# A four-layer graph network kernel: neighbour rows added in PSUM by VectorE, relation one-hots on ScalarE, two node tiles moved from the dense to the gathered side

## The reference

```
# layer 1, twice; nbrs holds the 32 neighbours of every node
h = crelu(h @ W.T + b)                      # complex: 128 real and 128 imaginary columns
out = w[0] * h
for k in range(deg): out = out + w[1 + k] * h[nbrs[:, k]]
# layer 2, per edge
a = hs @ Ws.T + h[dst] @ Wd.T + emb_rel[etype] @ Wr.T
e = leaky_relu((a @ attn_fc2_w.T)[:, 0], 0.01)
```

## Time and profile before

| | us |
|---|---|
| median of 3 runs (9929.73 to 9936.26) | 9930.99 |
| the profiled execution, its own time | 9934.95 |
| its span in the trace | 9932.5 |
| mean granted clock of TensorE, share of full speed | 0.743 |

### The profile page before, as it was taken

The page is one execution under the profiler, slowest core; times in us unless marked ns, Lnnn a source line. Parts: engine busy times, 40 slices in busy tenths (PEclk is TensorE's granted clock), DMA queues, the critical chain, the costliest instruction groups (busy, mean ns, idle before and its releaser), DMA issues.

```text
span 9932.5 us, 177577 instructions
## 1 busy us (share of the span) xinstructions
PE 7686.7 (77%) x39475; PEld 6071.9 (61%) x39475; DVE 8136.9 (82%) x24716; ACT 5907.6 (59%) x18248; POOL 6764.0 (68%) x7572
## 2 busy tenths in 40 slices
PE   4444445555799998888889999888888888848998
PEld 3333444444477777766667777666666666636775
DVE  7776666666888887999978888788888888899999
ACT  6777777777977773111100006588888888846665
POOL 0377777777088887666657777666666666649994
PEclk8555565555899999999999999755555555667666
DMA  2222222222688888777766662322222222210000
GB/s 53 52 54 53 52 53 53 53 53 53 220 240 242 238 238 270 270 278 264 265 225 237 243 237 79 85 49 49 50 50 50 49 49 49 49 27 1 1 1 27
DMA packets 533201, 1157.64 MB, mean 117 GB/s; under 512 B 148671, under 2 KB 400003, under 8 KB 511823
## 3 DMA queue, kind: packets, MB, share of 16 engines
q0 software_dynamic: 244944, 483.52, 20.3%
q10 hardware_dynamic: 22752, 517.02, 13.2%
q1 hardware_dynamic: 264478, 145.75, 5.6%
HBM read 892.96 MB, written 259.26 MB: 116 GB/s over the span
## 4 chain that ended last, share of the span: by engine, by line
DVE 30%; PE 21%; POOL 17%; issue 14%; ACT 12%; DVEq 2%; DMA 2%; SPq 1%; ACTq 0%; POOLq 0%
POOL onehot L2199 9%; PE banks L1428 7%; PE banks L2056 4%; POOL step_data L1464 4%; ACT banks L1190 3%; DVE banks L1726 3%; DVE keys L1486 3%; POOL gather_ring L1464 3%; PE banks L2066 2%; PE banks L1054 2%; DVE keys L1114 2%; ACT onehot L1043 2%; DVE keys L1123 2%; ACT onehot L1041 2%; DVE keys L2036 2%
## 5 line engine op out<-in xcount | busy, mean ns | idle before, releaser
L1029 POOL DMA_INDIRECT gather_ring<-mean_rows,step_data x1660 | 1597.5, 962 | 743.9 <-issue 317.2
L1054 PE MATMUL banks<-gather_ring,onehot 128*128 128x130 f32 x3320 | 958.8, 450 | 1120.8 <-DVE arena L1087 916.3
L1428 PE MATMUL banks<-arena 128*128 128x384 bf16 x8428 | 1617.6, 332 | 29.5 <-DMA arena<-split_out 26.6
L1428 PE MATMUL banks<-arena,keys 128*128 128x384 bf16 x8330 | 1579.2, 329 | 10.2 <-DMA arena<-split_im 10.2
L1054 PEld LDWEIGHTS banks<-gather_ring,onehot 128*128 128x128 f32 x3320 | 791.1, 300 | 1283.9 <-issue 1001.7
L1428 PEld LDWEIGHTS banks<-arena 128*128 128x128 bf16 x8428 | 1167.8, 139 | 295.3 <-issue 61.4
L1428 PEld LDWEIGHTS banks<-arena,keys 128*128 128x128 bf16 x8330 | 1149.2, 138 | 258.3 <-issue 28.3
L1464 POOL DMA_INDIRECT step_data<-hidden,window_idx x888 | 1002.9, 1129 | 391.4 <-issue 252.1
L1757 POOL DMA_INDIRECT step_data<-next_rows,window_idx x992 | 942.9, 951 | 402.4 <-issue 290.6
L1980 POOL DMA_INDIRECT gather_ring<-attention_rows,step_data x834 | 786.7, 943 | 416.3 <-PE banks L2056 271.2
L1980 POOL DMA_INDIRECT keys<-attention_rows,step_data x826 | 779.2, 943 | 387.2 <-PE banks L2056 286.9
(11 more groups left out here) (311 smaller groups left out, 19099.9 us busy)
## 6 DMA issues: line engine op xcount, KB each, us to landing
keys<-count_rows ACTq DMA_DIRECT2D x50, 3136.0 KB
arena<-count_rows ACTq DMA_DIRECT2D x50, 3136.0 KB
count_rows<-arena ACTq DMA_DIRECT2D x26, 3136.0 KB
count_rows<-keys ACTq DMA_DIRECT2D x26, 3136.0 KB
gather_ring<-mean_rows,step_data POOLq DMA_INDIRECT x1660
step_data<-next_rows,window_idx POOLq DMA_INDIRECT x992
step_data<-hidden,window_idx POOLq DMA_INDIRECT x888
gather_ring<-attention_rows,step_data POOLq DMA_INDIRECT x834
```

The lines of the kernel that those rows point to most:

```text
L1029: e.indirect_dma_start(ring_at(rings.slot(name, i), SUM_COLS, SUMS - 1), None, rows, bass.IndirectOffsetOnAxis(src_idx[:, i:i + 1], 0), bo ...
L1054: e.matmul(pass_bank[i % N_SUM_BANKS][:, 0:SUMS], onehot[:, i % STEP_SLOTS, :], ring_at(rings.slot(name, i), SUM_COLS, SUMS), start=True, ...
L1428: m = e.matmul(pass_bank[n % 2][:, 0:SPLIT_COLS], counts[t % 2][:, :, h], split[:, h, :], start=(h == 0), stop=(h == NODE_TILES - 1))
```

## The change

Five things change together.

1. `DENSE` goes from 52 to 50: 48 tiles are gathered in the first sum, 50 are dense. `ROUND` goes from 1664 to 1600 hops. The second sum still has 67 dense and 31 gathered tiles, so its late part builds the counts of 17 tiles in place of 15.
2. No DMA adds where it lands: every gathered tile has 8 batches of 4 rows, 384 in all, and 1536 gathers in place of 1472. By the new table 209 batches and 26 ends fall in round one.
3. `add_batch` replaces the reduction of each batch. A row pair (512 columns) of the batch is added to `gather_sum`, a whole PSUM bank: one instruction for a tile's first batch, two for each other. Once a tile a reduction folds the bank into the tile's sum. The second sum does the same (four rows of 128 columns side by side).
4. The bank comes from the count copies: `count_bank` has three banks in place of four.
5. The relations: `rel_scalar` on ScalarE makes relu(1 - |r - type|) in bf16, two instructions a relation into one of two buffers. VectorE does one instruction a relation, hot * score + sum, in PSUM, and one copy at the end. All 200 relations stand in the second sum, before its late part.

```diff
-DENSE = 52
-FOLDED = 23
+DENSE = 50
...
-EARLY_RELATIONS = 70
+REL_LAG = 8
...
+FIRST_BATCHES = [(j, g) for j in range(GATHERED) for g in range(DEG // ACCS)]
...
-    costs = list(itertools.accumulate(5 if rounds_of(i) == 2 else 2 for i in range(len(FIRST_BATCHES))))
-    for i, (j, g, n) in enumerate(FIRST_BATCHES):
-        time = (costs[i] + 4) * sum(PACE) * ROUND // (costs[-1] + 6)
+    total = len(FIRST_BATCHES)
+    for i, (j, g) in enumerate(FIRST_BATCHES):
+        time = (i + 3) * sum(PACE) * ROUND // (total + 3)
...
+    gather_sum = pass_bank[2]
...
-    picked = banks[:, 2 * BANK_WORDS:2 * BANK_WORDS + STEPS]
+    score_sum = banks[:, 3 * BANK_WORDS:3 * BANK_WORDS + STEPS]
+    type_hot = [keys_all[:, i * (STEPS // 2):(i + 1) * (STEPS // 2)].bitcast(BF16) for i in range(2)]
...
-    count_bank = [pass_bank[2], pass_bank[3], tile_bank[0], tile_bank[1]]
+    count_bank = [pass_bank[3], tile_bank[0], tile_bank[1]]
...
-        if b >= 4:
-            e.wait_ge(counted, b - 3)
+        if b >= len(count_bank):
+            e.wait_ge(counted, b - len(count_bank) + 1)
...
     def first_gpsimd(e):
         e.wait_ge(steps_saved, 32)
-        for i in range(len(FIRST_BATCHES) + 1):
-            if i < len(FIRST_BATCHES):
-                first_round(e, i, 0)
-            if i and rounds_of(i - 1) == 2:
-                first_round(e, i - 1, 1)
+        for i, (j, g) in enumerate(FIRST_BATCHES):
+            if i >= FIRST_SLOTS:
+                e.wait_ge(batch_summed, i - FIRST_SLOTS + 1)
+            for a in range(ACCS):
+                at = (g * ACCS + a) * GATHERED + j
+                e.indirect_dma_start(first_rows(i)[:, a, :], None, hidden1,
+                                     bass.IndirectOffsetOnAxis(gather_idx[:, at:at + 1], 0),
+                                     bounds_check=None).then_inc(rings.landed("first", i)[0], 16)
+
+    def add_batch(e, done, tiles, first, rows):
+
+        if first:
+            if tiles:
+                e.wait_ge(tile_folded, tiles)
+            e.tensor_tensor(gather_sum, rows[:, 0, :], rows[:, 1, :], ALU.add).then_inc(batch_summed)
+        else:
+            e.wait_ge(batch_summed, done)
+            e.tensor_tensor(gather_sum, rows[:, 0, :], gather_sum, ALU.add).then_inc(batch_half)
+            e.wait_ge(batch_half, done - tiles)
+            e.tensor_tensor(gather_sum, rows[:, 1, :], gather_sum, ALU.add).then_inc(batch_summed)
...
-        e.tensor_reduce(to, first_rows(i).rearrange("p r c -> p c r"), AX.X, ALU.add).then_inc(batch_summed)
-        if g:
+        add_batch(e, i, j, g == 0, first_rows(i).rearrange("p (h r) c -> p h (r c)", h=2))
+        if g == DEG // ACCS - 1:
+            if j >= 2:
+                e.wait_ge(mix_steps, MIX * PLACE[DENSE + j - 2] + 6)
             e.wait_ge(batch_summed, i + 1)
-            e.tensor_tensor(rows_sums[:, j % 2, :], rows_sums[:, j % 2, :], rows_sum, ALU.add).then_inc(batch_added)
+            e.tensor_reduce(rows_sums[:, j % 2, :], gather_sum.rearrange("p (r c) -> p c r", r=2), AX.X,
+                            ALU.add).then_inc(tile_folded)
...
         for r in range(RELATIONS):
-            own().tensor_scalar(picked, edge_type[:, 0:STEPS], float(r), rel_score[:, r:r + 1], ALU.is_equal,
-                                ALU.mult).then_inc(n.sem, n.up())
-            own().tensor_tensor(edge_score, edge_score, picked, ALU.add).then_inc(n.sem, n.up())
-            yield
+            hot, score = type_hot[r % 2], rel_score[:, r:r + 1]
+            e.wait_ge(rel_near, r + 1)
+            if r == 0:
+                e.tensor_scalar(score_sum, hot, score, None, ALU.mult).then_inc(n.sem, n.up())
+            else:
+                own().scalar_tensor_tensor(score_sum, hot, score, score_sum, ALU.mult, ALU.add).then_inc(n.sem, n.up())
+            yield
+        own().tensor_copy(edge_score, score_sum).then_inc(n.sem, n.up())
...
+    def rel_scalar(e):
+
+        e.wait_ge(built, ROUND)
+        for r in range(RELATIONS):
+            hot, number = type_hot[r % 2], iota_row[:, r:r + 1] if r < P else iota_rest[:, r - P:r - P + 1]
+            if r >= 2:
+                e.wait_ge(rel_steps.sem, r - 1)
+            e.activation(hot, edge_type[:, 0:STEPS], ACT.Abs, bias=number, scale=-1.0).then_inc(rel_far)
+            e.wait_ge(rel_far, r + 1)
+            e.activation(hot, hot, ACT.Relu, bias=ones[:, 0:1], scale=-1.0).then_inc(rel_near)
+            yield
...
-        weave(first_vector(e), itertools.islice(relations, EARLY_RELATIONS), 2 * ROUND + HOT_AHEAD, EARLY_RELATIONS,
-              ROUND + HOT_AHEAD + GROUPS)
-        weave(window2_vector(e), relations, ROUND - 2 * HOT_AHEAD, RELATIONS - EARLY_RELATIONS)
+        for _ in first_vector(e):
+            pass
+        weave(window2_vector(e), rel_vector(e), ROUND - 2 * HOT_AHEAD, RELATIONS, REL_LAG)
...
-        window2_scalar(e)
+        weave(window2_scalar(e), rel_scalar(e), ROUND - 2 * HOT_AHEAD - REL_LAG, RELATIONS)
```

More of the change, by code:

```diff
@@ L159, in ending2 @@
     return None if q is None else (q, ORDER2[q])
-def first_batches():
-    batches = []
-    for j in range(GATHERED):
-        n = DEG // (ACCS * (2 if j < FOLDED else 1))
-        batches.extend((j, g, n) for g in range(n))
-    return batches
-def rounds_of(i):
-    return DEG // (ACCS * FIRST_BATCHES[i][2])
+FIRST_BATCHES = [(j, g) for j in range(GATHERED) for g in range(DEG // ACCS)]
 def due(now, hop, total, stride):
@@ L269 @@
 PLACE = {t: q for q, t in enumerate(ORDER)}
-FIRST_ENDS = [i for i, (_, g, n) in enumerate(FIRST_BATCHES) if g == n - 1]
 DENSE_BY = list(itertools.accumulate(t < DENSE for t in ORDER))
@@ L427, in program @@
     gathered = [sem(f"gather_landed{i}") for i in range(GATHER_SLOTS)]
-    rings = Rings(gathered, (("mean", GATHER_SLOTS, [1] * STEPS), ("first", FIRST_SLOTS, [ACCS * rounds_of(i) for i in range(len(FIRST_BATCHES))]),
+    rings = Rings(gathered, (("mean", GATHER_SLOTS, [1] * STEPS), ("first", FIRST_SLOTS, [ACCS] * len(FIRST_BATCHES)),
                              ("second", BATCH_SLOTS, [BATCH] * SECOND * BATCHES),
@@ L724, in prep_vector_program @@
         own().tensor_copy(iota_half[:, :], row_int).then_inc(n.sem, n.up())
+        own().tensor_scalar(iota_rest[:, :], row_int[:, 0:RELATIONS - P], float(P), None, ALU.add).then_inc(n.sem, n.up())
         own().tensor_copy(ident_half[:, :], ident[:, :]).then_inc(n.sem, n.up())
@@ L1452, in first_rows @@
         return room[:, at * ACCS * 2 * D:(at + 1) * ACCS * 2 * D].rearrange("p (r c) -> p r c", r=ACCS)
-    def first_round(e, i, r):
-        j, g, n = FIRST_BATCHES[i]
-        if r:
-            sem_, value = rings.landed("first", i)
-            e.wait_ge(sem_, value - 16 * ACCS)
-        elif i >= FIRST_SLOTS:
-            e.wait_ge(batch_summed, i - FIRST_SLOTS + 1)
-        for a in range(ACCS):
-            k = (g * rounds_of(i) + r) * ACCS + a
-            e.indirect_dma_start(first_rows(i)[:, a, :], None, hidden1,
-                                 bass.IndirectOffsetOnAxis(gather_idx[:, k * GATHERED + j:k * GATHERED + j + 1], 0),
-                                 bounds_check=None, compute_op=ALU.add if r else ALU.bypass).then_inc(
-                rings.landed("first", i)[0], 16)
@@ L1742, in program @@
         "p (s r c) -> p s r c", s=BATCH_SLOTS, r=BATCH)
-    batch_sum, tile_sums = gather_ring[:, GATHER_WORDS - 3 * D:GATHER_WORDS - 2 * D], [
-        gather_ring[:, GATHER_WORDS - (2 - i) * D:GATHER_WORDS - (1 - i) * D] for i in range(2)]
+    tile_sums = [gather_ring[:, GATHER_WORDS - (2 - i) * D:GATHER_WORDS - (1 - i) * D] for i in range(2)]
     def second_gpsimd(e):
```

51 lines of the change are left out of this document (22 added, 29 removed).

## The result

The changed kernel takes 9619.33 us (median, 9616.33 to 9621.33) beside 9933.62 (9929.73 to 9937.54) for the kernel before on the same chip: ratio 0.9683, with a 95% interval of 0.9667 to 0.9700. The profiled execution took 9620.59 us, with a span of 9618.8.

A forecast was written before the change was run, and what follows sets the result against it. TensorE and GpSimd fill round one, VectorE bounds round two, gathers the second sum's first part. Terms -15 - 194 - 74 + 45 + 2 = -236 us on 9931 give 9695, range 9625 to 9825 (8 in 10).

The forecast's parts named there:

- Unit prices: Whole kernel: addition 0.73 us, fold 1.05, ScalarE's instruction 1.68, VectorE's relation instruction 2.0, plain gather 1.25 with issue.
- what was allowed for waits: Added over needs, in us: round one 37, 10 and 12, round two 50, second sum's first part 35.
- third count bank: Round one: TensorE's count matmul waits for the copy three groups before, not four; 10 us (0 to 50).
- a VectorE at 90%: Round one: VectorE needs 1039 of 1148 us, its cover for counts shrinks to about 110; 12 us added.
- 50 us were added: Round two: TensorE (879 us) and GpSimd (875) need the same and wait in order; 50 us (10 to 110).
- 35 us were added: Second sum's first part: for GpSimd and TensorE, which now meet at each tile's norm; stage 895 us.
- The rule on reductions: Reductions of batches at 1.22 us instead of 1.964: VectorE 1105 of 1148 us in round one, 50 added, 9745 in all.
- That the second sum runs on the pair ScalarE, VectorE: Second sum: VectorE and ScalarE wait for each other's relations; first part 977 us, 9777; pooled rivals 9750 to 9850, 0.28.
- the rival that ended slower: Second sum: two buffers give no overlap, first part 1130 us in place of 895; total 9930; chance above 9951: 0.05.
- Dear additions: Additions cost 1.0 us: round one 1215 (+67), 9762 in all; with costly handovers or late transfers 9750 to 9850: 0.28.
- Transfers that bind in round two: Round two: DMA about 90% busy, gathers land late, 45 to 90 us; 9740 to 9785; pooled rivals 9750 to 9850, 0.28.
- It is better than that: Waits of only 10 us in round two and 10 in the second sum: 9630; better than 9650: 0.13.

The follow-up runs named there:

- reduce_kept: The changed kernel with the first sum's batches reduced with a stride again; 9754.94 us beside 9942.25 for the kernel before, ratio 0.9811.
- rel_alone: The kernel before with only the relations moved (item 5), all 200 in the second sum; 9727.10 us beside 9942.25, ratio 0.9783.
- after_again: The changed kernel, unedited, run again; 9626.67 us beside 9944.13 for the kernel before, ratio 0.9681.
- folded: The changed kernel with 24 of 48 gathered tiles using DMAs that add where they land; ratios to the kernel before 1.0083, 1.0058, 1.0034, 1.0052.
- dense52: The changed kernel with 52 dense tiles in the first sum in place of 50; ratios to the kernel before 1.0144 and 1.0128.
- the long pairs: Timings of an edited kernel beside the kernel before in which the latter took 11273 to 11416 us, 13 to 15% more.
- ring4: The changed kernel with four slots of gathered rows in the first sum in place of five; ratios to the kernel before 1.0194 and 1.0184.

## Where the prediction failed, and what of it held

**Direction, bound and mechanism** held; the size did not. VectorE's busy time in round two was to be 583 us and is 577; TensorE's wait for the mixing went from 152.5 to 25.5; the second sum's first part is set by its gathers.

**Unit prices** held. An addition 0.69 (0.73 taken), ScalarE's pair 1.67 and 1.68 (1.68), the instruction of a relation 1.946 (2.0), a plain gather 0.95 and 0.30 of issue (the same; 0.98 in round one). The fold cost 0.692, the lower bound, where 1.05 was taken.

**The step that failed is what was allowed for waits.** By the prediction's prices TensorE needs 1089 us in round one, 879 in round two, and the gathers 860 in the first part. Measured stages are 1125, 900 and 874. So 36, 21 and 14 us are left over these needs, in place of the 59 (37 + 10 + 12), 50 and 35 that I added. These are 23 + 29 + 21 = 73 of the 78 us (314 less 236) by which the forecast was too high. Not all of what is left is waiting: TensorE is idle for 26 us of round one and for 17 of round two; the rest is work priced a little low.

- Round one, third count bank: 10 us were added. ScalarE's wait for a free counts buffer is nearly that of the earlier trace rows, 39.9 there:

```profile
ACT arena L1411 <- PE banks L1419: 38.0, 24, 3.0
...
PE banks L1405 <- DVE keys L1397: 6.9, 19, 0.9
```

  The second row is TensorE's wait for one-hots: 7 us, where 12 were added for a VectorE at 90% (it is at 88%). Before, with VectorE at 81%, this wait was 14 us, so it did not grow at all. So no more is left than the 37 us of before, and both additions were too much. A third of it is the one wait of 12.2 us on the border of the rounds, which the prediction did not name. reduce_kept shows that VectorE costs something at 95%: TensorE waits 83 us for one-hots. Between 88 and 95% nothing was measured.
- Round two: 50 us were added since TensorE and GpSimd have the same need. TensorE sets the round, with 78% of the chain in its dense matmuls, and 21 us are left over its need. GpSimd waits 23 us for VectorE in all (13.0 at the ring slots in `step_data`, 10.2 at those in `gather_ring`). The prediction had a case before it that spoke for less: it took 3% from round one as a stage where nobody else was full, but by its own count GpSimd needed 1160 of the 1163 us there. So two engines with the same need had cost 3% already, 28 us of 929. That the ring of batches and the end, a tile away, are what hides the rest was not tested.
- First part: 35 us were added for TensorE and GpSimd, who meet at each tile's norm; 14 are left, of which 10 are GpSimd's waits for VectorE and 4 three gathers more than the 688 counted. TensorE waits 30 us for the norm there (16.5 and 13.3), but the stage is GpSimd's. rel_alone was 25 below its expectation for the same reason, so it isn't the additions that gave them back.

**The late part** was 388 in place of 385, the gap 31 in place of 33.

**The rule on reductions.** With 1.964 us for 1024 strided columns I set the trace against the Trainium skill (VectorE: DVE Perf Modes, the perf-mode tier table), which gives a reduction one element a cycle wherever it reads. For the batch from SBUF the trace goes on to disagree: 1.967 in reduce_kept, so a batch went from 1.97 + 0.43 us to 1.38 and saved 1.02; by the rule it would have been 1.22 + 0.43, and the saving 0.27. The 115 us that reduce_kept lost in round one go with the first. For the fold out of PSUM the trace agrees with the rule: 0.692 us for 512, the price of an addition of 512. Whether it is the place, SBUF or PSUM, or the number of rows that makes the difference in the first sum was not tested apart; the second sum's fold, four rows of 128 out of PSUM, takes 0.692 us too.

**Rivals.** That the second sum runs on the pair ScalarE, VectorE: no. VectorE waited 37 us for one-hots, and the three instructions of a relation are 6% of the chain, where gathers and issue are 65%. With it falls the rival that ended slower, 1130 us for a first part that took 874. The Trainium skill (ScalarE: Activation LUTs, rules for kernel authors) gives simple arithmetic (relu, max, min, add, mul) to VectorE; here the comparison was moved off VectorE and item 5 alone gave 215 us, with ScalarE at 78% in the first part. Dear additions: no, 0.69. Transfers that bind in round two: the DMA share rose from 0.75 to 0.87, as the rival said, but VectorE's waits for gathered rows there are 1.2 us and those for other landed data 15, so it did not decide. "It is better than that" is the one that came, with waits of 21 and 14 us where it had 10 and 10.

**What is shown and what is not.** The ratios add up: item 5 alone 0.9783 (216 us of 9934), with items 1, 2, 4 and the second sum's additions 0.9811 (28 back), with the first sum's additions 0.9683 (127 more). The last figure agrees with the stages: 115 in round one and 10 in round two. The first and second are measured beside the same kernel before, the third beside another, and after_again repeated it (0.9681). How the 28 split between fewer dense tiles, plain gathers and the third bank is not shown. The first part's step from 915 to 875 us is there in reduce_kept too, so the first sum's additions have no part in it; the profile has 723 gathers in that stage of rel_alone and 691 in that of reduce_kept, and 32 fewer at 1.25 us are the 40 us. The two dense tiles fewer take 32 us off TensorE in the same stage, and no run parts the two. What the end of the adding DMAs alone brings was not shown either: folded has no pair like the result's, and neither has the old split of the tiles (dense52).

## What to carry to other kernels

When two engines are both near the bound of a stage, price their needs one by one from rows, and then take the larger; add for waits only what rows show now, from a stage that is really alike. Here a second engine at 96% (GpSimd in round two) left 2% of the stage over, and VectorE, which feeds TensorE in small steps, cost 14 us at 81%, 7 us at 88% and 83 us at 95%. The shares of the chain say which of two full engines sets the stage. Look first for work on the bounding engine that isn't tied to the stage: taking the relations off VectorE was two thirds of the gain, and the rest needed cheaper batches before more gathering could pay. A reduction over a strided view in SBUF was dear for its size here (1.97 us for 1024 columns), and two plain additions of the same elements were cheaper (1.38 us).

## What the runs showed of the hardware

- VectorE's reduction with a stride between the summed elements takes 1.967 us for 1024 f32 columns out of SBUF, 1.9 ns a column, but 0.692 us for 512 out of PSUM, 1.35 ns a column with the fixed part in it, as an addition does.
- An addition with an operand and the result in the same PSUM bank is not slower than one with both operands in SBUF (0.685 to 0.696, beside 0.689).
- In the long pairs the time of the single instructions stayed (gathers 0.95 us, additions 0.69), but engines stood idle for some us again and again for no cause that the trace has. Two rows of the waits of dense52, whole span (in the kernel after the first is 41.1 us and the second has no row):

```profile
PE banks L1045 <- issue: 461.8, 136, 6.2
PE banks L1419 <- issue: 325.1, 429, 3.2
```

  Work was also taken up later: in round two VectorE's first copy of a finished dense tile (it waits for a load as well), where VectorE stood idle before it, began 0.14 us after the tile's last matmul in the kernel after (median), and 3.3 to 6.5 us after it in the profiles of dense52, rel_alone_c, folded_d, reduce_kept_c and ring4_d. TensorE's mean clock in round two is 0.85 in the row of folded above. The preparation, the same in all kernels, was some 340 us longer. Round one took 1182 to 1223 us in rel_alone and folded, which have DMAs that add where they land, and 1437 to 1475 us in dense52, reduce_kept and ring4, which have plain gathers alone. What disturbs the long pairs, and why it strikes some kernels more, was not found; chip 4 gave both kinds of pair.
- One of the five executions of after_again, the profiled one, took 11080 us in place of 9626 to 9629. Its preparation is as long as ever (2711 us), but round one took 1635 us, round two 1318. TensorE was busy throughout, and the granted clock stood at 0.65 all through both sums, but for 0.5 in the 7 us between the rounds and in the gap. So 0.65 is no mean of the two levels, 0.5 and 1.0, that are the only ones in every other trace here. Why it was granted is not shown. The row is of 3050 to 4688 us, most of round one and the start of round two:

```profile
3050.00:4688.00 1638.00, 1634.68 (x6620) 1003.34 (x6619) 944.43 (x2810) 656.45 (x1427) 822.35 (x855) 0.65 0.53 187
```
